# A cross-attention kernel whose engines all get a new order for the same instructions

## What is computed

```python
# 16 batches, S = 512 queries and 512 keys, D = 512, H = 16 heads of DH = 64
Q = (x @ Wq + bq); K = (c @ Wk + bk); V = (c @ Wv + bv)        # then split into heads
scores = einsum('bhqd,bhkd->bhqk', Q, K) / sqrt(64) * mask     # masked scores are 0, not -inf
attn = softmax(scores, axis=-1)
ctx = einsum('bhqk,bhkd->bhqd', attn, V)
out = x + ctx @ Wo + bo
return (out - mean) * rsqrt(var + 1e-5) * gamma + beta
```

## Time and profile before

| | |
|---|---|
| median of 3 runs (lowest, highest) | 2347.05 us (2345.76 to 2347.08) |
| span of the profiled execution | 2344.9 us |
| TensorE busy | 2185.3 us, 93% |
| VectorE busy | 2020.0 us, 86% |
| ScalarE busy | 1788.3 us, 76% |
| GpSimd busy | 1055.4 us, 45% |
| mean granted TensorE clock | 0.968 |
| DMA | 363.28 MB, mean 155 GB/s |

### The profile page before, as it was taken

The page is one execution under the profiler, slowest core; times in us unless marked ns, Lnnn a source line. Parts: engine busy times, 40 slices in busy tenths (PEclk is TensorE's granted clock), DMA queues, the critical chain, the costliest instruction groups (busy, mean ns, idle before and its releaser), DMA issues.

```text
span 2344.9 us, 46357 instructions
## 1 busy us (share of the span) xinstructions
PE 2185.3 (93%) x12348; PEld 883.0 (38%) x12348; DVE 2020.0 (86%) x4283; ACT 1788.3 (76%) x3809; POOL 1055.4 (45%) x1576
## 2 busy tenths in 40 slices
PE   3689999999999999999999999999999999999985
PEld 1233434334343443434344343434434343343432
DVE  5778888989889898988989888898988989898891
ACT  3668697887869788796977868698786978878691
POOL 2125263453636345353634536354363635436343
PEclk9799999999999999999999999999999999999997
DMA  5358779787877868687796878878677887868683
GB/s 211 86 104 166 149 146 192 139 178 142 165 158 145 196 135 170 146 168 167 139 191 136 171 146 163 177 137 192 135 162 155 156 183 145 184 131 166 131 148 86
DMA packets 1117594, 363.28 MB, mean 155 GB/s; under 512 B 1073504, under 2 KB 1073504, under 8 KB 1117408
## 3 DMA queue, kind: packets, MB, share of 16 engines
q1 hardware_dynamic: 1114288, 361.58, 75.0%
q10 hardware_dynamic: 3120, 0.01, 0.1%
HBM read 76.30 MB, written 16.78 MB: 40 GB/s over the span
## 4 chain that ended last, share of the span: by engine, by line
PE 78%; ACT 9%; DVE 5%; issue 4%; POOL 2%; SPq 1%; DMA 1%; ACTq 0%; DVEq 0%; POOLq 0%
PE fill_ps L405 17%; PE fill_ps L406 16%; PE fill_ps L407 16%; PE ctx_ps L479 15%; PE score_ps L458 13%; ACT probs L640 4%; ACT p L654 3%; DVE score_ps L989 2%; ACT xT L608 1%; ACT v L619 1%; DVE p L1003 1%; DVE v L1024 1%; POOL neg_max L1325 0%; DVE small L873 0%; PE ctx_ps L392 0%
## 5 line engine op out<-in xcount | busy, mean ns | idle before, releaser
L640 ACT ACTIVATE probs<-score_ps,neg_max 128x512 f32<-128x512 f32 x1024 | 699.6, 686 | 297.5 <-POOL neg_max L1325 261.9
L989 DVE CUSTOM_DVE_ANT_0 score_ps<-score_ps,mask_sb,small 128x512 f32<-128x512 f32 x1024 | 753.2, 753 | 171.4 <-PE score_ps L458 166.6
L1003 DVE SCALAR_TENSOR_TENSOR p<-probs,inv_sum,p 128x512 f16<-128x512 f32 x896 | 774.2, 881 | 9.0 <-ACT p L654 7.0
L654 ACT ACTIVATE p<-probs,inv_sum 128x512 f16<-128x512 f32 x1024 | 705.1, 721 | 92.7 <-DVE inv_sum L997 87.4
L1325 POOL TENSOR_SCALAR neg_max<-row_max 128x2 f32<-128x2 f32 x512 | 185.4, 362 | 856.3 <-DVE row_max L989 853.0
L458 PE MATMUL score_ps<-k,q 64*128 64x512 f16 x3072 | 434.2, 381 | 41.7 <-ACT probs L640 41.7
L479 PE MATMUL ctx_ps<-pT,v 128*64 128x512 f16 x3072 | 393.1, 410 | 41.0 <-DVE v L1024 26.1
L479 PEld LDWEIGHTS ctx_ps<-pT,v 128*64 128x64 f16 x3072 | 177.4, 117 | 247.8 <-issue 106.9
L458 PEld LDWEIGHTS score_ps<-k,q 64*128 64x128 f16 x3072 | 121.9, 94 | 320.8 <-issue 128.0
L640 ACT ACTIVATION_READ_ACCUMULATOR probs<-score_ps,neg_max 128x1 f32 x1024 | 206.7, 202 | 0.0
L405 PE MATMUL fill_ps<-wv,cT 128*128 128x512 f16 x512 | 195.8, 382 | 6.0 <-DVE q L1018 6.0
(11 more groups left out here) (91 smaller groups left out, 2838.3 us busy)
## 6 DMA issues: line engine op xcount, KB each, us to landing
raw<-in_xt SPq DMA_DIRECT2D x64, 256.0 KB, 3.2
raw<-in_ct SPq DMA_DIRECT2D x64, 256.0 KB, 3.3
mask_sb<-in_mask_Bx1xSxS_fk SPq DMA_DIRECT2D x64, 256.0 KB, 3.2
acc<-in_x SPq DMA_DIRECT2D x64, 256.0 KB, 3.0
out<-acc SPq DMA_DIRECT2D x64, 256.0 KB, 2.4
pT<-p SPq DMA_TRANSPOSE x512, 4.4
...
```

The lines of the kernel that those rows point to most:

```text
L640: nc.scalar.activation(probs[:, i % E_TILES, :], score_ps[:, i % 4, :], ACT.Exp, bias=neg_max[:, p % 2, i:i + 1], accum_out=row_sum[:, p % ...
L654: nc.scalar.activation(p16[:, q, a, 0, :], probs[:, i % E_TILES, :], ACT.Copy, scale=inv_sum[:, p % 2, i:i + 1]).then_inc(p_rounded, 1)
L989: nc.vector.tensor_tensor_reduce(out=score_ps[:, i % 4, :], in0=score_ps[:, i % 4, :], in1=mask_sb[:, q, :], scale=score_scale, scalar=-3. ...
L1003: nc.vector.scalar_tensor_tensor(out=p16[:, q, a, 1, :], in0=probs[:, i % E_TILES, :], scalar=inv_sum[:, p % 2, i:i + 1], in1=p16[:, q, a, ...
```

## The change

The same instructions stand in another order in all five body functions. No instruction, buffer or wait of the loop is added or removed. The table FILL_BANK follows the new order of the fills, as does the list of bank users that a loop pass starts with. value_scale for batch 0 is called in the opening, and the call in the common order returns at once for it. For TensorE, one loop pass reads (' is the next batch, - the one before; S3.01 is scores(3, 0) and scores(3, 1); PV is values; brackets hold fills that follow each other):

The bank table:

```diff
 FLOOR = 1.0e-30
 
 FILL_BANKS = 3
-FILL_BANK = dict(zip("Q3 O1 V3 O2 K3 O3 K4 Q4 K5 Q5 Q6 K6 Q7 V4 K7 V5 V6 V7 Q0 K0 Q1 K1 Q2 V0 K2 O0 V1 V2".split(),
+FILL_BANK = dict(zip("K3 Q3 V3 K4 O1 Q4 O2 O3 K5 Q5 Q6 K6 Q7 K7 V4 V5 V6 V7 Q0 Q1 K0 K1 Q2 K2 V0 V1 O0 V2".split(),
                      (0, 1, 2, 0, 1, 2, 0, 1, 2, 0, 1, 2, 0, 1, 2, 0, 1, 2, 0, 1, 2, 0, 1, 2, 0, 1, 2, 1)))
 BOUND_COL = 16
 W_COL = {"q": 0, "k": 4, "v": 8, "o": 24}
```

The same on TensorE as a diff:

```diff
@@ -490,96 +474,86 @@
                     sum_first_bound(1)
                 if here is not None and not first:
                     users.update((FILL_BANK[f"{kind}{k}"], fill_read(here - 1 + ahead, kind, k))
-                                 for kind, k, ahead in (("K", 2, 1), ("V", 2, 1), ("V", 1, 1)))
-                if here is not None:
+                                 for kind, k, ahead in (("V", 0, 1), ("O", 0, 0), ("V", 2, 1)))
+                if here is not None:
+                    fill(here, "K", 3)
                     fill(here, "Q", 3)
+                    scores(here, 2, range(2, 4))
+                    fill(here, "V", 3)
+                    fill(here, "K", 4)
                 if prev is not None:
                     fill(prev, "O", 1)
                 if here is not None:
-                    fill(here, "V", 3)
-                    scores(here, 2, range(2, 4))
+                    scores(here, 3, range(0, 2))
+                    values(here, 0)
+                    fill(here, "Q", 4)
+                    scores(here, 3, range(2, 4))
                 if prev is not None:
                     fill(prev, "O", 2)
-                if here is not None:
-                    fill(here, "K", 3)
-                    values(here, 0)
-                    scores(here, 3, range(0, 2))
-                if prev is not None:
                     fill(prev, "O", 3)
                 if here is not None:
-                    scores(here, 3, range(2, 3))
-                    fill(here, "K", 4)
-                    fill(here, "Q", 4)
-                    scores(here, 3, range(3, 4))
+                    scores(here, 4, range(0, 2))
                     fill(here, "K", 5)
-                    scores(here, 4, range(0, 1))
+                    values(here, 1)
+                    scores(here, 4, range(2, 4))
                     fill(here, "Q", 5)
-                    scores(here, 4, range(1, 2))
-                    values(here, 1)
-                    scores(here, 4, range(2, 3))
                     fill(here, "Q", 6)
-                    scores(here, 4, range(3, 4))
+                    scores(here, 5, range(0, 2))
                     values(here, 2)
-                    scores(here, 5, range(0, 1))
                     fill(here, "K", 6)
-                    scores(here, 5, range(1, 2))
+                    scores(here, 5, range(2, 4))
                 if nxt is not None:
                     bound_inputs(nxt)
                 if here is not None:
                     fill(here, "Q", 7)
-                    scores(here, 5, range(2, 3))
+                    fill(here, "K", 7)
+                    scores(here, 6, range(0, 1))
                     values(here, 3)
-                    scores(here, 5, range(3, 4))
+                    scores(here, 6, range(1, 2))
                     fill(here, "V", 4)
-                    scores(here, 6, range(0, 1))
-                    fill(here, "K", 7)
-                    scores(here, 6, range(1, 2))
+                    scores(here, 6, range(2, 3))
                     fill(here, "V", 5)
-                    scores(here, 6, range(2, 3))
+                    scores(here, 6, range(3, 4))
                     fill(here, "V", 6)
-                    scores(here, 6, range(3, 4))
                     fill(here, "V", 7)
                     scores(here, 7, range(0, 2))
+                if nxt is not None:
+                    fill(nxt, "Q", 0)
+                if here is not None:
                     values(here, 4)
                 if nxt is not None:
-                    fill(nxt, "Q", 0)
-                if here is not None:
-                    scores(here, 7, range(2, 3))
+                    fill(nxt, "Q", 1)
+                if here is not None:
+                    scores(here, 7, range(2, 4))
                 if nxt is not None:
                     fill(nxt, "K", 0)
-                if here is not None:
-                    scores(here, 7, range(3, 4))
+                    fill(nxt, "K", 1)
+                if here is not None:
                     values(here, 5)
                 if nxt is not None:
-                    fill(nxt, "Q", 1)
-                    scores(nxt, 0, range(0, 1))
-                    fill(nxt, "K", 1)
-                    scores(nxt, 0, range(1, 2))
-                if here is not None:
-                    values(here, 6)
+                    scores(nxt, 0, range(0, 2))
                 if opening:
                     sum_weight_rows("v")
                     sum_first_bound(2)
                 if nxt is not None:
-                    scores(nxt, 0, range(2, 3))
                     fill(nxt, "Q", 2)
-                    scores(nxt, 0, range(3, 4))
+                if here is not None:
+                    values(here, 6)
+                if nxt is not None:
+                    scores(nxt, 0, range(2, 4))
+                    fill(nxt, "K", 2)
                     fill(nxt, "V", 0)
-                    scores(nxt, 1, range(0, 1))
-                    fill(nxt, "K", 2)
-                    scores(nxt, 1, range(1, 2))
+                    scores(nxt, 1, range(0, 2))
+                    fill(nxt, "V", 1)
                 if here is not None:
                     values(here, 7)
                 if nxt is not None:
-                    scores(nxt, 1, range(2, 3))
+                    scores(nxt, 1, range(2, 4))
                 if here is not None:
                     fill(here, "O", 0)
                 if nxt is not None:
-                    scores(nxt, 1, range(3, 4))
-                    scores(nxt, 2, range(0, 1))
-                    fill(nxt, "V", 1)
                     fill(nxt, "V", 2)
-                    scores(nxt, 2, range(1, 2))
+                    scores(nxt, 2, range(0, 2))
                 if opening:
```

GpSimd, from pair 5's last sums to pair 7's first negations:

```diff
+                    scale_sums(here, 5, 1)
+                if nxt is not None:
+                    split_input(nxt, "x", range(0, 1))
                 if here is not None:
                     negate_max(here, 6, range(0, 1))
-                    scale_sums(here, 5, 1)
-                if nxt is not None:
-                    split_input(nxt, "x", range(0, 1))
+                if nxt is not None:
+                    split_input(nxt, "x", range(1, 2))
+                    scale_biases(nxt)
                 if here is not None:
                     negate_max(here, 6, range(1, 2))
                 if nxt is not None:
-                    split_input(nxt, "x", range(1, 3))
+                    split_input(nxt, "x", range(2, 3))
                 if here is not None:
                     scale_sums(here, 6, 0)
                     negate_max(here, 6, range(2, 3))
+                if nxt is not None:
+                    split_input(nxt, "x", range(3, 4))
+                if here is not None:
+                    negate_max(here, 6, range(3, 4))
                     split_probs(here, 5, range(7, 8))
-                    negate_max(here, 6, range(3, 4))
-                if nxt is not None:
-                    scale_biases(nxt)
-                    split_input(nxt, "x", range(3, 4))
+                if nxt is not None:
                     split_input(nxt, "c", range(0, 1))
                 if here is not None:
-                    negate_max(here, 7, range(0, 1))
                     scale_sums(here, 6, 1)
                 if nxt is not None:
-                    split_input(nxt, "c", range(1, 3))
-                if here is not None:
-                    negate_max(here, 7, range(1, 2))
-                if nxt is not None:
-                    split_input(nxt, "c", range(3, 4))
+                    split_input(nxt, "c", range(1, 2))
+                if here is not None:
+                    negate_max(here, 7, range(0, 2))
+                if nxt is not None:
+                    split_input(nxt, "c", range(2, 4))
```

The flag of value_scale:

```diff
-            def value_scale(n):
+            def value_scale(n, early=False):
+                if is_first(n) and not early:
+                    return
```

599 lines of the change are left out of this document (255 added, 344 removed).

## The result

The changed kernel takes 2424.05 us (median of 4 runs, 2422.3 to 2428.34); the kernel before took 2346.41 beside it. The ratio is 1.0335 [1.0322, 1.0347]: 78 us slower, where 98 us faster had been forecast.

A forecast was written before the change was run, and what follows sets the result against it. TensorE was taken as the bound; 1.5 us from changes of shape, 2.1 from the clock and 2.9 from waits made 6.5 a batch, times 15 batches 98 us, so 2347 - 98 = 2249 us, range 2212 to 2328.

The forecast's parts named there:

- TensorE is the bound: In the steady part at least, TensorE bounds the kernel: 93% busy and 78% of the chain that ended last.
- Changes of shape, 1.5 us a batch: On TensorE, switches between fill, scores and values fall from 59 to 44 a batch, 0.10 us each, all on the path.
- Waits, minus 2.9 us a batch: TensorE's waits, 3.8 us a batch, lose three quarters, 2.9 us, mostly those around pair 7.
- The wait for the V split ahead of values(4): TensorE's 1.46 us wait ahead of pair 4's values pass gets 2.7 us more cover from Q0.
- Fifteen batches alike: The first batch and the loop's 14 have the full form; each gains 6.5 us, 98 us in all.
- Clock, minus 2.1 us: TensorE's slow clock behind long waits, 2.1 us a batch, goes if these waits go.
- rival F: Many short waits take TensorE's clock down: ten short waits a batch, 290 us slower, some 2640 us; chance 0.03.
- VectorE and GpSimd holding each other up, 7.3 us a batch: Where both read two SBUF tensors, VectorE's probability splits average 881 ns instead of 750, 56 a batch.
- VectorE is no bound yet: VectorE's 123.6 us would be 94% of a 131.7 us batch; the next bound, but 116 us without contention.
- B: Rival: the wait only moves and the clock falls as before; only changes of shape gain, 22 us, 2325 us; chance 0.22.
- A: The main forecast: 5 to 8 us a batch gained, 2249 us, range widened to 2222 to 2290; chance 0.57.
- D: Rival: queries two by two need all four score banks, TensorE waits at ten places a batch; 2385 us; chance 0.04.

The follow-up runs named there:

- after_unrolled: The changed kernel with its 14 loop passes written out, waits on constants and the increments behind them gone: 2312.43 us, 0.9856 of the kernel before.
- before_unrolled: The kernel before with its loop written out in the same way, orders unchanged: 2326.75 us, 0.9910 of the kernel before.

## Why the prediction was wrong

**TensorE is the bound: it was, and the change ended that.** This is the premise on which the sum stood. The prediction took the chain's 78% as a property of the kernel. It is one of the order. The chain of after_unrolled by engine, and of before_unrolled:

```profile
PE 53%; DVE 19%; POOL 10%; ACT 10%; issue 7%; DMA 1%; POOLq 0%; ACTq 0%; DVEq 0%; SPq 0%
```

```profile
PE 78%; DVE 15%; ACT 3%; POOL 2%; issue 1%; DMA 1%; SPq 0%; POOLq 0%; ACTq 0%; DVEq 0%
```

The old order keeps TensorE's matmuls in the chain, so that a late engine elsewhere is mostly covered; in the new one scores, mask, negation, exponential and scores again follow each other closely, and a delay in the round more often arrives at TensorE.

**Changes of shape, 1.5 us a batch: held.** Runs in a batch fall from 60 to 45 (the small bound matmul counted), and two queries in one go take 1.40 us: one begins at 1105.36 and the next fill at 1106.76.

```profile
1105.36 1.47 PE L442 MATMUL score_ps<-k,q 64*128 64x512 f16 x12
...
1106.76 0.39 PE L389 MATMUL fill_ps<-cT,wk 128*128 128x512 f16 x1
```

**Waits, minus 2.9 us a batch: wrong in sign.** This is the step that failed: TensorE's idle time was to fall by 2.9 us a batch and rose by 5.5, from 3.9 to 9.4. The wait for the V split ahead of values(4) went, as argued. But the waits for exponentials rose from 23 to 108 us over 1659 us. I had looked only at the two places where TensorE waited before and checked whether they had more cover, not how much slack the places had that didn't wait. Part of the rise is at the jump: 3.1 us of the 9.6 that TensorE's matmuls wait in 1092.9 to 1237.7 us. The rest is spread over short waits, as at pair 7's first queries:

```profile
1203.93 5.38 DVE L939 SCALAR_TENSOR_TENSOR p<-probs,inv_sum,p 128x512 f16<-128x512 f32 x4
...
1204.73 1.36 POOL L1217 TENSOR_TENSOR cT<-raw,cT 128x512 f16<-128x512 f32 x1 [0.18 <-POOL raw L1214]
...
1205.12 0.69 ACT L614 ACTIVATE probs<-score_ps,neg_max 128x512 f32<-128x512 f32 x1 [1.09 <-DVE p L939]
...
1206.68 0.69 ACT L614 ACTIVATE probs<-score_ps,neg_max 128x512 f32<-128x512 f32 x1 [0.78 <-DVE p L939]
...
1207.51 0.39 PE L442 MATMUL score_ps<-k,q 64*128 64x512 f16 x1 [0.74 <-ACT probs L614]
...
1208.61 0.82 PE L442 MATMUL score_ps<-k,q 64*128 64x512 f16 x5 [0.71 <-ACT probs L614]
```

Four splits of VectorE in a row take 5.38 us. The exponentials write into a ring of eight tiles and wait for these splits to free them, and the scores wait for the exponentials. The prediction followed the score banks and never this ring. The ring isn't the main part, though: ScalarE's exponentials wait 26.3 us for these splits in 476 to 2135 us, 23.3 before, and 217 us for negated maxima, 195 before. Both together grew by 24 us, TensorE's waits by 85. That the rest comes from a shorter distance between TensorE's scores and the exponentials that free their banks is argued; no run isolates it.

**Terms that the sum didn't have.** The loop's jump appears in the prediction only where changes of shape are counted "the wrap included". It cost the new order 67 us and the old one nothing. In the old order TensorE is busy all 8 us of 1079 to 1087, with ScalarE's branch at 1080.22 and VectorE's at 1083.14. The increments behind waits, 40 against 17 us, were likewise not priced; the 4% of "issue" in the earlier trace rows, 1% in before_unrolled, was the trace's sign of such costs. Written out, jump and increments gone, the new order gains 112 us and the old one 20; the 92 between are more than the 78 by which the changed kernel is slower.

**Fifteen batches alike: wrong.** The sum took one figure for the first batch and the 14 of the loop. The 14 later stretches lost 91 us, 6.5 each, and the two ends gained some 16 in all.

**Clock, minus 2.1 us: wrong as given, right in mechanism.** 2.6 us a batch before, 2.2 in the changed kernel, 0.2 in after_unrolled: it goes with the long waits, and the long wait had moved to the jump. Short waits alone did not take it down: in after_unrolled TensorE waits 88 times, at most 1.1 us, and the clock is lost for 0.2 us a batch. This goes against rival F.

**VectorE and GpSimd holding each other up, 7.3 us a batch: right as a reading, open in its worth.** Before, 540 of the 896 splits have no operation of 512 columns of GpSimd beside them and take 746 ns; the 254 beside its two-input operations alone take 1167. So (881 - 746) x 56 = 7.6 us a batch is the time above the undisturbed split. The change was to leave or shrink it, and it stayed (mean 879, undisturbed 741); written out it grew (926). Not all of it hangs on the subtractions: without them the mean is 866 ns in the new order and 812 in the old. What counted at GpSimd was, as far as the runs tell, its own time between negations and sums. "VectorE is no bound yet" held as a statement on its sum (88% at most in the kernels that compute everything), but it is 19% of the chain of after_unrolled.

**Rivals.** Written out, the order on its own comes near B's figure: the wait moves (49 us in 1659, after 45 before), and of the 22 us that B gives 14 come, measured against the old order in the same form. That is luck in part: B keeps the slow clock and gets 1.5 us in each batch, and here the clock is nearly at full level (0.2 us lost a batch, 2.1 in before_unrolled), the middle batches gain 0.2 to 0.4 us each, and the 14 us come from the two ends. A's 2249 is reached, at 2251.5, only with the jump, the increments and GpSimd's subtractions out of the way. D, slower through scores that wait for their banks when queries go two by two, had a chance of 0.04 and the right kind of wait: 143 of them in 1659 us, 108 us or 9.5 a batch, and D's dear case was ten of 0.9. With the jump announced 71 us of them are left; written out, 46, and 24 with the queries taken apart. Its price of 38 us isn't where the 78 come from, as it knew no jump and no increments. What stays open: why just this order has so little slack in the round, beyond the places shown, how much of it is the pairing, and what contention costs in all.
